# Graph network, last edge stage: 18432 of 106496 edge slots gathered row by row by GpSimd, the other 88064 looked up on TensorE in 43 turns

## What is computed

```python
def gcn_conv(x, W, b, src, dst, n):
    xw = x @ W
    ...
    norm = dinv[s] * dinv[d]
    out = jax.ops.segment_sum(norm[:, None] * xw[s], d, num_segments=n)
    return out + b
h = gcn_conv(x, W1, b1, src, dst, n)
h = jax.nn.relu(batch_norm(h, g1, be1))
z = batch_norm(gcn_conv(h, W2, b2, src, dst, n), g2, be2)
return z @ Wd + bd
```

## Time and profile before

| | |
|---|---|
| median of 3 runs | 5474.11 us (5472.19 to 5474.27) |
| the profiled execution | 5473.0 us, span 5471.2 us |
| PE busy over the span | 4466.7 us, 82% |
| DVE / ACT / POOL busy | 3910.2 / 2035.2 / 3260.2 us |
| mean granted TensorE clock | 0.892 of full speed |
| edges_pairs begins / ends | 5096 / 5471.2 us |

### The profile page before, as it was taken

One profiled execution on the slowest core, in us unless ns is written; L12 is line 12 of the kernel. 1 busy time (PEld: TensorE's weight loads), 2 busy tenths in 40 slices (PEclk: granted clock), 3 DMA queues, 4 the chain that ended last, 5 costly groups with the idle time before them and its releaser, 6 DMA issues. The chain is left out here.

```text
span 5471.2 us, 107262 instructions
## 1 busy us (share of the span) xinstructions
PE 4466.7 (82%) x25109; PEld 3562.5 (65%) x25109; DVE 3910.2 (71%) x8497; ACT 2035.2 (37%) x3851; POOL 3260.2 (60%) x3351
## 2 busy tenths in 40 slices
PE   5999999999895888888876555555567899997993
PEld 4888888888675888888865555555565566664331
DVE  5999999999764888888878444444456677777673
ACT  3666666666425555656544100000021000000670
POOL 2777777777315776777720677777746777775003
PEclk8999999999996888989987777777778999999896
DMA  6333333333234555555535333333343211111333
GB/s 202 111 102 104 104 104 103 103 104 104 80 115 117 126 127 125 129 127 127 126 82 164 101 110 109 109 109 109 106 144 96 40 39 38 35 35 20 89 124 94
DMA packets 449153, 560.08 MB, mean 102 GB/s; under 512 B 208325, under 2 KB 316793, under 8 KB 448681
## 3 DMA queue, kind: packets, MB, share of 16 engines
q0 software_dynamic: 149616, 374.73, 25.0%
q1 hardware_dynamic: 292226, 176.81, 11.9%
q10 hardware_dynamic: 6840, 3.36, 0.3%
HBM read 502.04 MB, written 59.34 MB: 103 GB/s over the span
## 5 line engine op out<-in xcount | busy, mean ns | idle before, releaser
L503 POOL DMA_INDIRECT l_rows<-tmp_tab,l_idx x832 | 881.9, 1060 | 376.5 <-issue 252.5
L1166 POOL DMA_INDIRECT l_rows<-tmp_tab,src_sb x832 | 791.3, 951 | 328.9 <-issue 235.8
L1886 POOL DMA_INDIRECT l_rows<-tmp_tab,src_sb x812 | 767.9, 946 | 253.1 <-issue 235.6
L1972 PE MATMUL l_psa<-l_sel,l_rows 128*128 128x128 f32 x3248 | 572.3, 349 | 411.1 <-issue 225.9
L1972 PEld LDWEIGHTS l_psa<-l_sel,l_rows 128*128 128x128 f32 x3248 | 531.0, 256 | 452.3 <-issue 261.7
L2112 POOL DMA_INDIRECT l_rows<-tmp_tab,src_sb x695 | 657.4, 946 | 235.6 <-issue 203.6
L801 PE MATMUL l_psw<-l_fw,l_ssp 128*128 128x256 f32 x3328 | 764.1, 383 | 0.0
L1912 DVE TENSOR_TENSOR acc<-acc,l_psa 128x256 f32 x832 | 351.0, 422 | 536.2 <-PE l_psa L1972 449.8
L801 PEld LDWEIGHTS l_psw<-l_fw,l_ssp 128*128 128x128 f32 x3328 | 617.5, 190 | 153.5 <-issue 77.2
L2215 PE MATMUL l_found<-l_tabs,l_hot 128*128 128x384 f32 (+1 forms) x1872 | 651.7, 502 | 0.0
L1486 PE MATMUL l_psa<-l_sel,l_rows 128*128 128x128 f32 x3328 | 603.8, 310 | 56.4 <-DVE acc L1386 55.0
(11 more groups left out here) (345 smaller groups left out, 7766.6 us busy)
## 6 DMA issues: line engine op xcount, KB each, us to landing
l_rows<-tmp_tab,src_sb POOLq DMA_INDIRECT x2339
l_edge<-in_edge_t SPq DMA_DIRECT2D x104, 256.0 KB
l_own<-tmp_tab SPq DMA_DIRECT2D x1280, 1.0 KB
l_own<-tmp_tab ACTq DMA_DIRECT2D x1280, 1.0 KB
l_own<-tmp_tab ACTq DMA_DIRECT2D x1280, 0.2 KB
l_own<-tmp_tab SPq DMA_DIRECT2D x1280, 0.2 KB
tmp_x<-n_X SPq DMA_DIRECT2D x39, 512.0 KB
n_X<-in_x SPq DMA_DIRECT2D x26, 512.0 KB
```

Of the source, the lines that this page charges most:

```text
L503: nc.gpsimd.indirect_dma_start(out=rows[r][:, t, :], out_offset=None, in_=table[:, :], in_offset=bass.IndirectOffsetOnAxis(ap=idx[q][:, j: ...
L1166: nc.gpsimd.indirect_dma_start(out=rows[r][:, j, :], out_offset=None, in_=dram["tab1"][:, :], in_offset=bass.IndirectOffsetOnAxis(ap=sh["s ...
L1886: nc.gpsimd.indirect_dma_start(out=rows[g % ROWS][:, t, :], out_offset=None, in_=table[:, :], in_offset=bass.IndirectOffsetOnAxis(ap=sh["s ...
L1972: last = nc.tensor.matmul(by_tile(g)[0:n, t, k * P:(k + 1) * P], left[:, f:f + n], sel[b][:, t, :], start=True, stop=True)
```

## The change

Of the 208 runs the last 36, 18432 edge slots, leave the turns. They are laid out anew as 128 lanes of 144 edges (`LONG`), one on each partition. The table is written to memory (`tab4`), and POOL fetches the two numbers of 128 edges with one indirect DMA, 144 of them, in windows of 16 of which up to two or three may be under way. `edges_gcn` makes the row numbers (`long_row`) and the flags of these lanes (`keep_long`). DVE scans the fetched numbers along each partition, once for the lanes' last sums and once, after the carry, for the sums themselves (`sum_long`), which SP writes behind the others in `sums`. The carry chain covers the 172 short and the 128 long lanes. The turns are 43, the quads 3, the depth of the byte buffers 6 where it was 4, while SP still waits for the masks by the same formula. The gathers at the last edges are 49 (`NT_REAL`) where they were 52.

```diff
-QUADS = -(-GROUPS // LANES)
+LONG = 144
+PAIRS = GROUPS - P * LONG // RUN
+QUADS = -(-PAIRS // LANES)
+CHAIN = max(PAIRS + P, QUADS * LANES)
+LONG_AT = PAIRS * RUN
...
-    "deg_row": [1, NP], "sums": [TILES * P, OC], "mix_row": [1, TILES * P],
+    "tab4": [NP, OC], "deg_row": [1, NP], "sums": [TILES * P, OC], "mix_row": [1, TILES * P],
...
-        first_r, prev_r, last_r = (ph.sb(n, [OC, QUADS * LANES], I32) for n in ("first_r", "prev_r", "last_r"))
+        first_r, prev_r, last_r = (ph.sb(n, [OC, CHAIN], I32) for n in ("first_r", "prev_r", "last_r"))
+        long_src, long_dst, long_prev, long_lo, long_hi = (ph.sb(f"long_{n}", [P, LONG], I32)
+                                                           for n in ("src", "dst", "prev", "lo", "hi"))
...
+                for off, tile in ((1, long_dst), (0, long_prev)):
+                    sp.dma_start(tile[:, :], flat[:, LONG_AT + off:LONG_AT + off + P * LONG].rearrange("a (p n) -> (a p) n", p=P)
+                                 ).then_inc(long_in, 16)
+                sp.dma_start(long_src[:, :], dram["src_flat"][:, LONG_AT:LONG_AT + P * LONG].rearrange("a (p n) -> (a p) n", p=P)
+                             ).then_inc(long_in, 16)
                 for quad in range(QUADS):
-                    k = min(KQ, (GROUPS - quad * LANES) // NB)
+                    k = min(KQ, (PAIRS - quad * LANES) // NB)
...
-                for off, tile in ((1, first_r), (0, prev_r), (RUN, last_r)):
+                for off, tile in ((1, first_r), (0, prev_r), (None, last_r)):
+                    near = RUN if off is None else off
+                    far = LONG_AT + (LONG if off is None else off)
                     for c in range(OC):
                         with nc.allow_non_contiguous_dma(reason="one destination of each run of edges"):
-                            sp.dma_start(tile[c:c + 1, 0:GROUPS], flat[:, off:off + (GROUPS - 1) * RUN + 1:RUN]
+                            sp.dma_start(tile[c:c + 1, 0:PAIRS], flat[:, near:near + (PAIRS - 1) * RUN + 1:RUN]
+                                         ).then_inc(dst_in, 16)
+                            sp.dma_start(tile[c:c + 1, PAIRS:PAIRS + P], flat[:, far:far + (P - 1) * LONG + 1:LONG]
                                          ).then_inc(dst_in, 16)
...
+                    dve.wait_ge(long_in, 48)
+                    nc.vector.tensor_tensor(keep_long[:, :], long_dst[:, :], long_prev[:, :], ALU.is_equal)
+                    nc.vector.tensor_scalar(long_lo[:, :], long_src[:, :], P - 1, None, ALU.bitwise_and)
+                    nc.vector.tensor_scalar(long_hi[:, :], long_src[:, :], 7, None, ALU.logical_shift_right).then_inc(long_done, 1)
+                    dve.wait_ge(long_done, 1)
+                    nc.vector.scalar_tensor_tensor(out=long_row[:, :], in0=long_lo[:, :], scalar=float(NT), in1=long_hi[:, :],
+                                                   op0=ALU.mult, op1=ALU.add).then_inc(long_done, 1)
+                    dve.wait_ge(long_done, 2)
+                    dve.wait_ge(dst_in, 16 * (2 * OC * NB * QUADS + 6 * OC))
...
-    BUFS = 4
+    BUFS = 6
+    TURNS = PAIRS // NB
+    SLABS = -(-CHUNKS // CT)
+    NT_REAL = -(-N // P)
+    WINDOW = 16
...
+        got, sum_long = ph.sb("got", [P, LONG, OC]), ph.sb("sum_long", [P, LONG, OC])
+        scan_long, into_long = ph.sb("scan_long", [P, OC, LONG]), ph.sb("into_long", [P, OC])
+        total, carry = ph.sb("total", [OC, CHAIN]), ph.sb("carry", [OC, CHAIN])
...
+                sp.wait_ge(setup, 2)
+                sp.dma_start(dram["tab4"].rearrange("(p t) c -> p (t c)", p=P), tab[:, 0:W]).then_inc(tab_out, 16)
...
-                with sp.Fori(1, ITERS // BUFS) as turn:
+                with sp.Fori(1, TURNS // BUFS) as turn:
                     for q in range(BUFS):
                         it = turn * BUFS + q
                         hold(sp, ph, masked, it * NB - NB)
                         load(it, q)
+                for q in range(TURNS % BUFS):
+                    it = TURNS // BUFS * BUFS + q
+                    hold(sp, ph, masked, it * NB - NB)
+                    load(it, q)
...
+                sp.wait_ge(long_done, 1)
+                sp.dma_start(dram["sums"][LONG_AT:LONG_AT + P * LONG, :].rearrange("(p n) c -> p (n c)", p=P),
+                             sum_long[:, :, :].rearrange("p n c -> p (n c)")).then_inc(stored, 16)
                 for quad in range(QUADS):
-                    n = min(LANES, GROUPS - quad * LANES)
+                    n = min(LANES, PAIRS - quad * LANES)
...
-                pool.wait_ge(stored, 16 * QUADS)
-                for t in range(NT):
+                pool.wait_ge(tab_out, 16)
+                for e in range(LONG):
+                    turn, at = e // WINDOW, e // WINDOW % 3
+                    if turn >= 2 and e % WINDOW == 0:
+                        pool.wait_ge(got_in[(turn - 2) % 3], 16 * WINDOW * ((turn - 2) // 3 + 1))
+                    nc.gpsimd.indirect_dma_start(
+                        out=got[:, e, :], out_offset=None, in_=dram["tab4"][:, :],
+                        in_offset=bass.IndirectOffsetOnAxis(ap=long_row[:, e:e + 1].bitcast(U32), axis=0),
+                    ).then_inc(got_in[at], 16)
+                pool.wait_ge(stored, 16 * (QUADS + 1))
+                for t in range(NT_REAL):
                     nc.gpsimd.indirect_dma_start(
                         out=node[:, t, :], out_offset=None, in_=dram["sums"][:, :],
                         in_offset=bass.IndirectOffsetOnAxis(ap=last_edge[:, t:t + 1].bitcast(U32), axis=0),
...
-                with act.Fori(0, ITERS // BUFS) as turn:
+                def one_hots(q, turn):
+                    it = turn * BUFS + q
+                    act.wait_ge(bytes_in[q], turn * 32 + 32)
...
+                with act.Fori(0, TURNS // BUFS) as turn:
                     for q in range(BUFS):
...
+                        one_hots(q, turn)
+                for q in range(TURNS % BUFS):
+                    one_hots(q, TURNS // BUFS)
...
-                with dve.Fori(0, ITERS // BUFS) as turn:
+                with dve.Fori(0, TURNS // BUFS) as turn:
                     for q in range(BUFS):
                         one_hot(q, turn)
                         for b in range(NB):
                             mask(q, turn, b)
+                for q in range(TURNS % BUFS):
+                    one_hot(q, TURNS // BUFS)
+                    for b in range(NB):
+                        mask(q, TURNS // BUFS, b)
...
+                nc.vector.memset(node[:, NT_REAL:, :], 0.0)
+                nc.vector.memset(psv[:, QUADS * RUN:CHUNKS * P], 0.0)
                 ch.link(last)
-                dve.wait_ge(reduced, ITERS + 2)
+                for i in range(3):
+                    dve.wait_ge(got_in[i], 16 * sum(e // WINDOW % 3 == i for e in range(LONG)))
+                for c in range(OC):
+                    nc.vector.tensor_tensor_scan(scan_long[:, c, :], keep_long[:, :], got[:, :, c], 0.0, ALU.mult, ALU.add)
+                dve.wait_ge(reduced, TURNS + 2)
                 for quad in range(QUADS):
                     last = nc.vector.tensor_tensor_scan(scan[:, quad, :], keep[:, quad, :], psv[:, quad * RUN:(quad + 1) * RUN],
                                                         0.0, ALU.mult, ALU.add)
                 ch.link(last)
                 nc.vector.tensor_tensor(spread[:, :, :], at_run[:, :].unsqueeze(1).to_broadcast([P, QUADS, LANES]),
                                         scan[:, :, RUN - 1:RUN].to_broadcast([P, QUADS, LANES]), ALU.mult).then_inc(ends_done, 1)
-                dve.wait_ge(ends_ps, 2)
+                dve.wait_ge(ends_ps, 3)
                 nc.vector.tensor_copy(col_t[:, :], psg[0:OC, RUN:RUN + P]).then_inc(carry_done, 1)
-                ch.link(nc.vector.tensor_tensor_scan(total[:, :], one[:, :], psg[0:OC, 0:QUADS * LANES], 0.0, ALU.mult, ALU.add))
+                ch.link(nc.vector.tensor_tensor_scan(total[:, :], one[:, :], psg[0:OC, 0:CHAIN], 0.0, ALU.mult, ALU.add))
...
-                nc.vector.tensor_tensor(carry[:, 1:], cont[:, 1:], total[:, 0:QUADS * LANES - 1], ALU.mult).then_inc(carry_done, 1)
-                dve.wait_ge(carry_ps, 1)
+                nc.vector.tensor_tensor(carry[:, 1:], cont[:, 1:], total[:, 0:CHAIN - 1], ALU.mult).then_inc(carry_done, 1)
+                dve.wait_ge(carry_ps, 2)
+                nc.vector.tensor_copy(into_long[:, :], psg[:, 2 * RUN + QUADS * LANES:2 * RUN + QUADS * LANES + OC])
...
+                for c in range(OC):
+                    last = nc.vector.tensor_tensor_scan(sum_long[:, :, c], keep_long[:, :], got[:, :, c], into_long[:, c:c + 1],
+                                                        ALU.mult, ALU.add)
+                last.then_inc(long_done, 1)
...
-                dve.wait_ge(fetched, 16 * NT)
+                dve.wait_ge(fetched, 16 * NT_REAL)
...
-                for it in range(ITERS):
+                for it in range(TURNS):
```

(47 more changed lines are left out.)

6 lines of the change are left out of this document (3 added, 3 removed).

## The result

| | before | changed |
|---|---|---|
| median | 5473.6 us (4 runs, 5472.19 to 5474.27) | 5420.87 us (4 runs, 5419.15 to 5421.61) |
| profiled execution / its span | 5473.0 / 5471.2 us | 5419.15 / 5417.4 us |
| POOL busy | 3260.2 us | 3395.0 us |
| mean granted TensorE clock | 0.892 | 0.892 |

The ratio is 0.9903 with a 95% interval of 0.9891 to 0.9916: 52.7 us less, where 46.9 were forecast. The median of 5420.87 lies in the stated range of 5420 to 5438, but only 0.9 us above its low end. The spans differ by 53.8 us.

What follows compares the result with a forecast made beforehand. PE's gapless turns were taken to bound the kernel; turns -41.6, tail -0.6, last gathers -3.7 and preparation -1.0 summed to -46.9 us, giving a median of about 5427 us, range 5420 to 5438.

Steps and rivals of the forecast that it cites:

- What bounds, and the turns: Last phase: PE bounds the turns without a gap at 4.627 us each; nine fewer turns save 41.6 us.
- The gathers are hidden: POOL's 144 gathers beside the turns: 1.248 us apart, landed at 5291.6, 12 us before DVE's need, costing nothing.
- I take no effect: Last few of the 144 gathers, meeting the loads of x: no delay assumed, as 8-byte rows need almost no transfer time.
- The far bound: Same meeting with the loads of x: gathers land only when x has landed, at 5308, 5 us past the need.
- rival 1: POOL ends last in the turns: slower gathers, 5432, or held for each one-hot, 5436; chance 0.14, the lock's share 0.05.
- The row of 0.08 us for each: Turns: each of 43 DVE one-hots slows a POOL gather by 0.08 us, 3.4 us in all, under the cover.
- Rival 2: Turns: the byte loads come late; 0.2 us a turn would cost 8.6 us, giving 5436; chance 0.03.
- The tail: From the turns to the gathers at the last edges: steps sum to -0.6 us, bounds -3 and +3.
- PE's added matmuls: Tail: a 128-column matmul for the long lanes' ends and a two-column one for their carry, +0.3 us.
- The gathers at the last edges: After the tail: 49 gathers in place of 52 at 1.248 us each, -3.7 us, certainly on the path.
- The preparation: SP's DMAs in edges_gcn ahead of the rows PE waits for: 6.05 us gone, new ones added, net -1.0 us.
- The sign given: edges_gcn in the changed profile: PE's wait for l_own would be about 12.9 us.

Runs made afterwards that it cites:

- e3: Changed kernel with lanes of 160 edges, so 160 gathers and 42 turns: 5430.84 us, ratio 0.9925 to the kernel before.
- e4: Changed kernel with lanes of 128 edges, so 128 gathers and 44 turns: 5426.57 us against 5416.54 of the changed kernel beside it.
- e5: Changed kernel without its 144 gathers and DVE's wait for them, the fetched numbers set to 0: 5419.57 us, ratio 0.9904 to the kernel before.
- e6: Changed kernel with all 63 loads of destinations in edges_gcn spread behind SP's first four row fetches: 5401.28 us, ratio 0.9874 to the kernel before.
- e1: Kernel before with 49 gathers at the last edges in place of 52: 5465.56 us against 5471.57, ratio 0.9989.
- e7: Changed kernel with 15 of SP's loads in edges_gcn put behind its first row fetch: 5413.57 us against 5416.54 of the changed kernel.
- e10: The kernel of e6 run once more, unaltered: 5404.97 us, ratio 0.9871 to the kernel before.
- e2: Kernel before with only the scratch table tab4 declared: 5467.74 us against 5471.57, ratio 0.9992.

## Why the prediction was right, point by point

- **What bounds, and the turns.** Right to the tenth: 4.63 us a turn, 41.6 us. e3 and e4 show it from both sides.
- **The gathers are hidden.** Right, as e5 shows: taken away, they give back at most 1.6 us, of which 1.5 lie in stretches that scatter. The cover was mis-sized, 5.7 us and not 12. The start was well placed (5105.5 in a phase that began 5.7 us earlier, so 5111 where 5110 was said), but the pitch was 1.261 and not 1.248, which is 1.9 us over 144. The larger part is the step "I take no effect" for the loads of x. Ahead of them a gather took 2.2 to 4.4 us to land (those issued up to 5200); SP issues the first load of x at 5279.38, and the six issued from 5279.4 on took 5.7 to 7.2. In e6 x starts at 5261.3, and the gathers issued from 5262.2 on took 5.7 to 6.6. The last one, issued at 5285.8, took 6.1 where 3.1 was reckoned and landed at 5291.9, 5.7 us ahead of DVE's need at 5297.6. The far bound, a landing only when x has landed, did not come about.
- **The lock of rival 1.** The row of 0.08 us for each was the better guide. In the changed kernel the longest gather is 1.110 us, 0.166 over the median, and the mean is 0.956 beside 0.943 for the undisturbed 49: 144 x 0.013 = 1.9 us, not 20.7. The Trainium skill (SBUF — State Buffer, Who interferes with whom) says that while DVE is in a two-port mode whoever starts first has the shared pair for the whole instruction and the other one blocks. No gather here waited as long as a whole one-hot of 0.481 us; whether these one-hots run in such a mode, no run shows. Both engines do show delays (DVE's one-hot up to 0.22 us longer, and not without the gathers). Between two gathers POOL is free for only 1.261 - 0.944 = 0.317 us, so each one-hot meets a gather; why the mean delay is so small was not tried.
- **Rival 2** did not come true, but its margin was misread. SP issued the last turn's low bytes at 5326.12 and ACT began to read them at 5334.09, 8.0 us later and not 13.9; in the changed kernel it is 8.1 (5278.51 to 5286.60). The deeper buffers gave nothing, as SP waits for the masks by the same formula.
- **The tail**, -2.7 where -0.6 was summed, inside its bounds. Two terms failed most. PE's added matmuls came at -0.4, not +0.3: from the first matmul of the carry to the scan over the lanes it was 1.63 us before (5350.75 to 5352.38) and 1.27 after (5302.15 to 5303.42). The first of them is narrower (192 columns for 256) and falls in a window with a granted clock of 0.72 (5302 to 5304) where it was 0.50 (5350 to 5352); it took 0.49 us for 1.01. And the turning round fell from 10.03 to 7.46, by 2.6 and not 1.7; the 0.9 beyond the forecast goes with the clock's earlier rise (last section), which is luck. Two smaller ones nearly cancel: the way to the quads' first scan +0.2 for +0.6, and the last store +0.5 for +0.2.
- **The gathers at the last edges**, -4.6 where -3.7 was said: e1 shows the missing 0.8 in the last landing, which I had taken as fixed.
- **The preparation**, -1.7 where -1.0 was said; SP's own part was -1.9. e7 and e6 show the mechanism, one for one and a little over. Two things were left out of the sum. The third quad's narrower DMAs issued in 3.18 and 3.09 us, where they had taken 4.02 and 3.70: -1.5. And the twelve `l_mix_b` loads behind the short ones took 6.99 us in place of 5.99: +1.0. The sign given, a wait of 12.9 us, did not show: it stayed at 13.9, as PE arrived earlier as well.
- **The 4 us ahead of edges_gcn** had no term. They may be scatter, as e6 and e10 differ there by 7.5 us, or in part placement (e2). In the profiled executions they are 4.0 of the 6.9 us that the spans fell beyond the forecast, and carried the time towards the low end of the range. Put right for them, the last part says 1333.6 - 1283.8 = 49.8 where 46.9 was forecast.
- **The end**, +1.0: the matmuls into `l_psv` before the output took 5.09 us where they had taken 4.31. That is the clock and not the change: it rose later into them (granted 0.59 from 5390 to 5392, against 0.79 from 5444 to 5446 before), and e2, with the matmuls of the kernel before, took 5.24. So this 0.8 is scatter that made the changed kernel slower, as the 0.9 of the turning round is scatter that made it faster.

## What to carry to other kernels

When work moves to an idle engine, compute the whole timeline of the new work (start, pitch, landing) against the moment at which it is needed, and try the next size on either side: here 144 was balanced within one step, and 160 threw away 11 of the 53 us. An issuing queue is an engine too: 63 loads needed over 400 us later stood ahead of one that PE was waiting for, and moving them added no work and gave 15 us. And compare stretches from a common mark rather than whole spans, as the phases ahead can drift by more than the effect.

## What was not expected of the hardware

The turning round on PE, the same 16 records, took 10.03, 8.94, 8.54 and 9.99 us in four profiles, and the 12 records 6.92 to 8.12 in the eight others. The windows tell why (stretch, length, PE, PEld, DVE, ACT, POOL busy, PEclk, DMA share, GB/s), here of the changed kernel:

```profile
5310.00:5312.00 2.00, 2.00 (x4) 0.50 (x3) 1.19 (x2) 0.00 (x0) 0.00 (x0) 0.50 0.00 0
5312.00:5314.00 2.00, 2.00 (x4) 0.51 (x3) 0.68 (x1) 0.63 (x1) 0.00 (x0) 0.72 0.00 0
5314.00:5316.00 2.00, 2.00 (x6) 0.55 (x4) 0.68 (x1) 0.63 (x1) 0.00 (x0) 1.00 0.61 131
```

PE starts at 5308.90 with the clock at 0.50 (1.2 GHz) after some 11 us in which it was mostly idle, and is granted 1.00 (2.4 GHz) from about 5313, 4 us into it; before the change the rise came about 6 us in the earlier trace rows. The moment moves from profile to profile, and with it up to 1.5 us of equal work in the turning round (8.54 to 10.03), 1.3 in the look-ups of the first two turns (8.73 to 10.02) and 1.1 in the matmuls into `l_psv` (4.29 to 5.34). A term smaller than that cannot be told in such a stretch from one profile.
